# Coupled attention: queries with their turned tanh in one stack of 128 rows, and one score product per four heads

## The reference

```python
Q = split_heads(x @ Wq.T + bq)
K = split_heads(x @ Wk.T + bk)
V = split_heads(x @ Wv.T + bv)
attn_scores = jnp.einsum('bhid,bhjd->bhij', Q, K) / scale
Qn = jnp.tanh(Q)
Kn = jnp.tanh(K)
QJ = jnp.einsum('bhid,hde->bhie', Qn, J_attn)
delta = jnp.einsum('bhie,bhje->bhij', QJ, Kn)
attn_scores = attn_scores + lambda_attn * delta
attn_probs = jax.nn.softmax(attn_scores, axis=-1)
out = jnp.einsum('bhij,bhjd->bhid', attn_probs, V)
```

## Time and profile before

| | |
|---|---|
| median of 3 runs | 2906.14 us (2905.02 to 2907.65) |
| the profiled execution | 2905.46 us, of which the span is 2903.7 us |
| mean granted TensorE clock | 0.886 of full |
| TensorE busy | 2287.8 us, 79% |
| VectorE busy | 1654.6 us, 57% |
| ScalarE busy | 1354.4 us, 47% |
| GpSimd busy | 673.9 us, 23% |
| the coupled stage | about 972 to 1275 us of the span |

### The profile page before, as it was taken

How to read it: one execution, slowest core, us unless ns; L and a number is a source line. 1 busy time by engine, 2 the same in 40 slices (tenths; PEclk the granted TensorE clock), 3 DMA queues, 4 the chain that set the end, 5 groups by cost and what they waited for, 6 DMA issues and landing times. The chain is left out here.

```text
span 2903.7 us, 49967 instructions
## 1 busy us (share of the span) xinstructions
PE 2287.8 (79%) x15043; PEld 1793.6 (62%) x15043; DVE 1654.6 (57%) x4694; ACT 1354.4 (47%) x3498; POOL 673.9 (23%) x772
## 2 busy tenths in 40 slices
PE   7689999589998788869999878877777677776550
PEld 5567777479997555547777756765555555555330
DVE  2357767658885566646766767444545454533313
ACT  2166667456664455537666734433333333333210
POOL 3100000101113100010000004244444444444534
PEclk9799999899999799989999999987888878878655
DMA  3066654227662100026666431444444343433542
GB/s 98 6 154 120 123 119 106 63 88 231 206 209 77 44 1 0 0 54 134 125 123 125 96 106 49 142 135 122 132 127 138 117 130 120 120 112 115 164 150 83
DMA packets 320714, 316.71 MB, mean 109 GB/s; under 512 B 71441, under 2 KB 299746, under 8 KB 320546
## 3 DMA queue, kind: packets, MB, share of 16 engines
q1 hardware_dynamic: 296514, 261.41, 34.0%
q0 software_dynamic: 24032, 53.25, 6.3%
HBM read 209.24 MB, written 105.32 MB: 108 GB/s over the span
## 5 line engine op out<-in xcount | busy, mean ns | idle before, releaser
L793 ACT ACTIVATE cross_pr<-cross_sc,cross_mn 112x375 f32<-112x375 f32 x512 | 310.4, 606 | 233.3 <-DVE cross_mn L883 232.5
L883 DVE CUSTOM_DVE_ANT_0 cross_sc<-cross_ps,cross_masked 112x375 f32<-112x375 f32 x512 | 272.8, 543 | 179.3 <-PE cross_ps L681 158.5
L2363 POOL DMA_INDIRECT switch_slots_x<-switch_ctx,switch_slot x256 | 247.8, 968 | 492.5 <-ACT switch_ctx L2534 422.4
L2470 PE MATMUL switch_ps<-switch_ow,switch_ct 128*128 128x256 f32 x672 | 221.9, 461 | 170.4 <-ACT switch_ct L2539 89.1
L2596 DVE SCALAR_TENSOR_TENSOR switch_vt<-switch_ps,switch_chosen,switch_vt 112x128 f32<-112x128 f32 x512 | 144.2, 344 | 364.8 <-remote 162.9
L104 PE MATMUL switch_ps<-switch_vw,switchgates_xh 128*112 128x512 f32 x512 | 226.6, 442 | 103.2 <-issue 48.2
L2375 POOL DMA_INDIRECT switch_fetched<-switch_slots_y,switch_slot x256 | 240.2, 938 | 200.8 <-DVE all_x L2633 72.9
L2470 PEld LDWEIGHTS switch_ps<-switch_ow,switch_ct 128*128 128x128 f32 x672 | 143.5, 225 | 226.9 <-ACT switch_ct L2539 109.4
L689 PE MATMUL cross_ps<-all_ident,cross_pr 112*125 112x112 f32 x1536 | 256.4, 276 | 23.5 <-DVE cross_pt L890 21.9
L689 PEld LDWEIGHTS cross_ps<-all_ident,cross_pr 112*125 112x125 f32 x1536 | 234.0, 190 | 45.0 <-DVE cross_pt L890 27.7
L2544 ACT COPY switch_y_out<-switch_ps 128x512 f32<-128x512 f32 x168 | 99.9, 595 | 287.8 <-remote 179.0
(11 more groups left out here) (409 smaller groups left out, 5506.4 us busy)
## 6 DMA issues: line engine op xcount, KB each, us to landing
experts_w_raw<-in_L_ffn_w_dram SPq DMA_DIRECT2D x42, 1024.0 KB, 5.5
switch_slots_y<-switch_y_out SPq DMA_DIRECT2D x168, 256.0 KB
cross_k<-cross_k_dram SPq DMA_DIRECT2D x96, 375.0 KB, 8.1
cross_k_dram<-cross_ks SPq DMA_DIRECT2D x32, 750.0 KB, 4.5
switch_rows_in<-switch_slots_x SPq DMA_DIRECT2D x168, 128.0 KB
switch_ow<-in_L_ffn_o_w_dram SPq DMA_DIRECT2D x168, 128.0 KB
all_place<-in_ctx_dram SPq DMA_DIRECT2D x32, 375.0 KB
cross_q<-cross_q_dram SPq DMA_DIRECT2D x192, 56.0 KB, 4.4
```

What stands on the lines that cost most here:

```text
L793: nc.scalar.activation(pr[:, h % NB, :], sc[:, h % NB, :], ACT.Exp, bias=mn[parity][:, h:h + 1], scale=-1.0, accum_out=rs[parity][:, h:h + ...
L883: nc.vector.tensor_tensor_reduce(out=sc[:, h % NB, :], in0=ps[0:T, SCORES + h % 2, 0:S2], in1=mask_of[:], scale=-0.25, scalar=3e38, op0=AL ...
L2363: pool.indirect_dma_start(out=slots_x[h % 2], out_offset=at, in_=ctx[n % 2][:, j, :], in_offset=None)\
L2470: last = nc.tensor.matmul(ps[:, TILE_Y, q * D:(q + 1) * D], ct[g % 2][:, q * P:(q + 1) * P], ow[g % RING][:], start=True, stop=True)
```

## The change

The two products of a score become one. Its 128 contracted rows now hold four heads instead of eight: 64 rows with the queries of the four heads and 64 with their turned and scaled tanh; on the other side 64 rows with keys and 64 with the keys' tanh. The tile `qk` [128, 2, 2, 2, 112] holds this for queries (index 0) and keys (index 1), chunks, and halves of a chunk (i). For half 0 the plain values stand in rows 0 to 63 and the tanh in rows 64 to 127, for half 1 the other way round; `J` is put into `Jd` shifted by 64 columns, so that the turned tanh come out in the rows where they are wanted.

- VectorE adds the biases of queries and keys, in two instructions of 64 rows x 448 elements, right behind the subtraction of group 1 (line 1289 of the new file), before the sum of group 0.
- ScalarE's tanh of the queries is two instructions of 64 rows x 224 (line 1198), of the keys two more (line 1201), in group 1. The masks are four copies of 128 rows x 448 elements with the head mask as scale (line 1207), in group 2, then the turned tanh in two halves (line 1214). `o` stays behind them.
- TensorE's `scores` is one product of 448 columns (line 1098). Its other instructions are as before.
- GpSimd builds the head mask with two more small operations. SyncE's loads are the same in number.

```diff
@@ tiles @@
-        head_mask = s.sb("head_mask", [P, HP])
+        head_mask = s.sb("head_mask", [P, 2, GH])
...
-        k32 = s.sb("k32", [P, DC, T])
         qn = s.sb("qn", [P, DC, T])
-        q = [s.sb(f"q{b}", [P, DC, T]) for b in range(2)]
-        qj = [s.sb(f"qj{b}", [P, DC, T]) for b in range(2)]
-
-        km = [s.sb(f"km{b}", [P, DC, HP, T]) for b in range(2)]
-        knm = [s.sb(f"knm{b}", [P, DC, HP, T]) for b in range(2)]
+        qk = [s.sb(f"qk{b}", [P, 2, DC, 2, T]) for b in range(2)]
+        km = [s.sb(f"km{b}", [P, DC, 2, GH, T]) for b in range(2)]
@@ SyncE: where J is put @@
-                sp.dma_start(Jd[r:r + HD, h // HP, r:r + HD], J[h]).then_inc(J_loaded, 16)
+                at = (r + HALF) % P
+                sp.dma_start(Jd[r:r + HD, h // HP, at:at + HD], J[h]).then_inc(J_loaded, 16)
@@ GpSimd: head mask @@
             c.link(pool.affine_select(out=head_mask[:], in_=head_mask[:], compare_op=ALU.is_ge, fill=0.0, base=0,
-                                      pattern=[[-HD, HP]], channel_multiplier=1))
-            pool.affine_select(out=head_mask[:], in_=head_mask[:], compare_op=ALU.is_ge, fill=0.0, base=HD - 1,
-                               pattern=[[HD, HP]], channel_multiplier=-1).then_inc(const_ready, 1)
+                                      pattern=[[-HALF, 2], [-HD, GH]], channel_multiplier=1))
+            c.link(pool.affine_select(out=head_mask[:], in_=head_mask[:], compare_op=ALU.is_ge, fill=0.0, base=HD - 1,
+                                      pattern=[[HALF, 2], [HD, GH]], channel_multiplier=-1))
+            pool.tensor_tensor(head_mask[:, 0, :], head_mask[:, 0, :], head_mask[:, 1, :], ALU.add).then_inc(const_ready, 1)
@@ TensorE: scores(b, parity, g) @@
                 if g == 0:
                     pe.wait_ge(k_ready, b + 1)
-                    pe.wait_ge(tanh_ready, 2 * b + 2)
                     pe.wait_ge(qj_ready, b + 1)
                 wait(pe, shifted, b * G + g - 1)
-                c, h = g * GH // HP, g * GH % HP
-                bank = ps[0:T, SCORES + g % 2, 0:GH * T]
-                nc.tensor.matmul(bank, q[parity][:, c, :], km[parity][:, c, h:h + GH, :].rearrange("p a b -> p (a b)"),
-                                 start=True, stop=False)
-                nc.tensor.matmul(bank, qj[parity][:, c, :], knm[parity][:, c, h:h + GH, :].rearrange("p a b -> p (a b)"),
-                                 start=False, stop=True).then_inc(s_done, 1)
+                nc.tensor.matmul(ps[0:T, SCORES + g % 2, 0:GH * T], qk[parity][:, 0, g // 2, g % 2, :],
+                                 km[parity][:, g // 2, g % 2].rearrange("p a b -> p (a b)"),
+                                 start=True, stop=True).then_inc(s_done, 1)
@@ ScalarE: front(b, parity, u) @@
-                    act.wait_ge(qk_done, b + 1)
-                    wait(act, k_ready, b)
-                    wait(act, tanh_ready, 2 * b)
-                    for m in range(DC):
-                        nc.scalar.activation(q[parity][:, m, :], bank0[:, m * T:(m + 1) * T], ACT.Identity,
-                                             bias=qk_bias[:, 0, m:m + 1])
-                    for m in range(DC):
-                        last = nc.scalar.activation(k32[:, m, :], bank0[:, (DC + m) * T:(DC + m + 1) * T], ACT.Identity,
-                                                    bias=qk_bias[:, 1, m:m + 1])
-                    last.then_inc(qk_ready, 1)
                     act.wait_ge(qk_ready, b + 1)
-                    nc.scalar.activation(qn[:], q[parity][:], ACT.Tanh).then_inc(tanh_ready, 1)
-                elif u in (2, 3):
-
-                    wait(act, s_done, (b - 1) * G)
-                    for h in range((u - 2) * HP // 2, (u - 1) * HP // 2):
-                        last = nc.scalar.activation(knm[parity][:, :, h, :], k32[:], ACT.Tanh, scale=head_mask[:, h:h + 1])
-                    if u == 3:
-                        last.then_inc(tanh_ready, 1)
+                    for i in range(2):
+                        rows_of = slice(i * HALF, (i + 1) * HALF)
+                        last = nc.scalar.activation(qn[rows_of], qk[parity][rows_of, 0, :, i, :], ACT.Tanh)
+                    last.then_inc(tanh_ready, 1)
+                    for i in range(2):
+                        last = nc.scalar.activation(qk[parity][(1 - i) * HALF:(2 - i) * HALF, 1, :, i, :],
+                                                    qk[parity][i * HALF:(i + 1) * HALF, 1, :, i, :], ACT.Tanh)
+                    last.then_inc(ks_ready, 1)
+                elif u == 2:
+                    act.wait_ge(ks_ready, b + 1)
+                    for h in range(GH):
+                        last = nc.scalar.activation(km[parity][:, :, :, h, :], qk[parity][:, 1], ACT.Copy,
+                                                    scale=head_mask[:, 0, h:h + 1])
+                    last.then_inc(k_ready, 1)
                 else:
                     act.wait_ge(j_done, b + 1)
-                    nc.scalar.activation(qj[parity][:].rearrange("p a b -> p (a b)"), bank0[:, 0:DC * T], ACT.Identity,
-                                         scale=lam4[:]).then_inc(qj_ready, 1)
+                    for i in range(2):
+                        rows_of = slice((1 - i) * HALF, (2 - i) * HALF)
+                        last = nc.scalar.activation(qk[parity][rows_of, 0, :, i, :],
+                                                    bank0[rows_of, 0:DC * T].rearrange("p (a b) -> p a b", a=DC),
+                                                    ACT.Identity, scale=lam4[rows_of])
+                    last.then_inc(qj_ready, 1)
@@ ScalarE: batch @@
-                        for u in ((), (1, 2), (4, 3), ())[g]:
+                        for u in ((), (1,), (2, 3), ())[g]:
@@ VectorE: front(b, parity, u) @@
-                    dve.wait_ge(qk_ready, b + 1)
-                    for h in range(HP):
-                        last = nc.vector.tensor_scalar(km[parity][:, :, h, :], k32[:], head_mask[:, h:h + 1], None, ALU.mult)
-                    last.then_inc(k_ready, 1)
+                    dve.wait_ge(qk_done, b + 1)
+                    for i in range(2):
+                        rows_of = slice(i * HALF, (i + 1) * HALF)
+                        last = nc.vector.tensor_tensor(
+                            qk[parity][rows_of, :, :, i, :],
+                            ps[rows_of, FRONT, 0:2 * DC * T].rearrange("p (n m t) -> p n m t", n=2, m=DC),
+                            qk_bias[rows_of].unsqueeze(3).broadcast_to([HALF, 2, DC, T]), ALU.add)
+                    last.then_inc(qk_ready, 1)
@@ VectorE: batch @@
                     shift(b, g, ch)
+                    if not last and g == 1:
+                        front(b + 1, 1 - parity, 1)
                     if g >= 1:
                         total(b, parity, g - 1)
...
-                    if not last and g in (1, 2):
-                        front(b + 1, 1 - parity, g - 1)
+                    if not last and g == 1:
+                        front(b + 1, 1 - parity, 0)
```

More of the change, by code:

```diff
@@ L956, in stage_coupled_attention @@
         HP = P // HD
+        HALF = P // 2
         w = [s.sb(f"w{n}", [P, DC, D]) for n in range(4)]
@@ L993, in stage_coupled_attention @@
         xs_ready, qk_done, v_done, j_done = (s.sem(n) for n in ("xs_ready", "qk_done", "v_done", "j_done"))
-        qk_ready, tanh_ready, v_ready, qj_ready, k_ready = (s.sem(n) for n in ("qk_ready", "tanh_ready", "v_ready", "qj_ready", "k_ready"))
+        ks_ready, tanh_ready, v_ready, qj_ready, k_ready = (s.sem(n) for n in ("ks_ready", "tanh_ready", "v_ready", "qj_ready", "k_ready"))
         s_done, shifted, exped, summed, t_done, pt_ready, pv_done = (
@@ L998, in stage_coupled_attention @@
         o_ready, y_done, var_ready, rstd_ready = (s.sem(n) for n in ("o_ready", "y_done", "var_ready", "rstd_ready"))
-        xn_ready, xt_done, xt_ready, chain = (s.sem(n) for n in ("xn_ready", "xt_done", "xt_ready", "chain"))
+        xn_ready, xt_done, xt_ready, chain, qk_ready = (
+            s.sem(n) for n in ("xn_ready", "xt_done", "xt_ready", "chain", "qk_ready"))
         CHAIN = G + 5
@@ L1085, in front @@
                 else:
-                    pe.wait_ge(tanh_ready, 2 * b + 1)
+                    pe.wait_ge(tanh_ready, b + 1)
                     if isinstance(b, int) and b == 0:
@@ L1267, in batch @@
                         tail(b - 1, 1)
-            for u in (0, 1, 2, 4, 3):
+            for u in range(4):
                 front(0, 0, u)
@@ L1338, in batch @@
                         tail(b - 1, 1 - parity, 0, ch)
-                    if not last and g in (1, 2):
-                        front(b + 1, 1 - parity, g - 1)
+                    if not last and g == 1:
+                        front(b + 1, 1 - parity, 0)
                     if before and g == 3:
                         tail(b - 1, 1 - parity, 1, ch)
-            for u in range(2):
+            for u in (1, 0):
                 front(0, 0, u)
```

## The result

The changed kernel takes 2947.99 us in the median of its runs (2939.28 to 2954.82), beside 2906.89 for the kernel before on the same chips. The ratio is 1.0124, 95% interval 1.0095 to 1.0153: slower by some 36 us by the ratio; the medians lie 41 apart. The profiled execution took 2939.28 us, its span 2937.4. It is the fastest of the four, so what follows explains 33.8 us.

A forecast was written before the change was run, and what follows sets the result against it. Each batch was taken as two legs ending in waits, not bound by TensorE throughout. From 2905.5 us, +5.2 (second leg) − 3.3 (first and last batch) + 17.7 (clock) gave 2925, range 2898 to 2944.

The forecast's parts named there:

- S0's saved work: First head group's scores: one product fewer saves 0.75 us, but TensorE's wait for the normalised row grows from 0.76 to 1.51.
- first leg: Batch part from output projection to S1: a latency through VectorE and GpSimd, nothing saved, 7.52 us again.
- VectorE's adds: Two bias adds ahead of group 0's sum, 0.54 us each, eat TensorE's saved 1.5; third group's maximum 4.79 after S1.
- S1: First score product of the second head group, where the prediction cuts a batch; the four groups' scores are numbered from zero.
- ScalarE's queue: Four masked copies (2.24 us) and turned tanh (0.68) ahead of `o`: `o` at 9.91, projection 10.29 after S1, +0.37 per batch.
- The clock: TensorE's idle lump of 2.9 us before the projection brings one clock fall per batch, 1.5 us each, +17.7 us net.
- First and last batch: Ends of the stage: first batch −2.0 us from saved products, last −1.3 without adds and copies, together −3.3.
- The walk to 6.0: Last batch, without adds and copies: the projection near 6.0 us after S1 instead of 7.30, −1.3.
- second leg: Batch part from S1 to the output projection, ending in a wait for `o`: 9.92 us becomes 10.29, +5.2 over 14 batches.
- The rival of two falls per batch: The 1.5 us wait behind the first group's scores brings a second clock fall per batch: 2951 us, chance 7%.
- The clock holds: Rival: clock falls stay at about two in the stage, as before: 2907 us, no measurable difference, chance 24%.
- The rival of the shorter queue: Copies 0.48 us each, turned tanh halves 0.34 together, clock held: projection 9.63 after S1, 2898 us, chance 15%.

The follow-up runs named there:

- experiment 5: The kernel before with the second score product (the tanh part) left out, all else computed as before: 2895.8 us, ratio 0.9966 to the kernel before.
- Experiment 2: The changed kernel with unread products filling TensorE's waits, three ahead of the projection, one behind the first group's scores: 2920.9 us, ratio 1.0058 to the kernel before.
- experiment 7: The changed kernel with ScalarE's copy `o` first and two of four masked copies moved behind the second group's tanh: 2858.2 us, ratio 0.988 to the kernel before.
- experiment 3: The changed kernel with unread products ahead of the projection only, one in one kernel, three in the other: 2918.6 and 2927.4 us, stages 326.7 and 326.2.
- experiment 6: The changed kernel with the four masked key copies as VectorE multiplies instead of ScalarE copies: 2899.1 us, ratio 1.0003 to the kernel before.
- experiment 1: The changed kernel with each score product computed twice into the same bank: 2936.6 us, ratio 1.013 to the kernel before.
- 4: The changed kernel with ScalarE's copy `o` moved ahead of the masked copies and the turned tanh: 2896.8 us, ratio 0.9968 to the kernel before.
- 8: On another chip: the kernel before with `o` ahead of the tanh, 2541.7 us, ratio 0.9974; and the kernel of experiment 7 again, 2513.1 us, ratio 0.9868.

## Why the prediction came out as it did

The time, 2948 in the median and 2939.28 in the profiled execution, lies above the forecast 2925, and slower was the likeliest side. The range ended at 2944: the profiled execution is inside it, the median 4 us above. The mechanism was right; its terms were too small, and the one for the first and last batch had the wrong sign, as follows.

- *S0's saved work, first leg unchanged.* Right: 7.49 in the one first leg at full clock (forecast 7.52), and 7.52 in experiment 5.
- *VectorE's adds.* Maximum of S2 at 4.92 after S1 (1084.53), forecast 4.79, with its own queue in front of it, as said. The two adds hold VectorE 1.25, so 0.63 each, not 0.54:

```profile
L1289 DVE TENSOR_TENSOR coupled_qk<-coupled_ps,all_qk_bias 64x448 f32<-64x448 f32 x20 | 12.3, 616 | 0.1
```

  The nearer price was the upper bound, the full 0.62 of L1301.
- *ScalarE's queue.* Third exponent 6.23 (6.11), copies from 7.12 and 2.37 for four instead of 2.24, turned tanh 0.80 instead of 0.68, `o` at 10.29 (9.91), projection at 10.67 (10.29). Three steps were each low by 0.12 to 0.13 us (VectorE's adds, the four copies, the turned tanh), all in one direction, and the leg came to +0.75 instead of +0.37. Over 13 batches that is +9.8, and the forecast had +4.8. Half of 128 rows saved nothing: a tanh of 64 rows by 224 elements takes 388 ns in the mean, as its 128-row kind did (0.39 in the earlier trace rows), and the two halves of the turned tanh 442 each, as the one of 128 rows did (0.44):

```profile
L1207 ACT ACTIVATE coupled_km<-coupled_qk,coupled_head_mask 128x448 f32<-128x448 f32 x41 | 24.1, 658 | 0.0
...
L1214 ACT ACTIVATE coupled_qk<-coupled_ps,all_lam 64x224 f32<-64x224 f32 x22 | 9.7, 442 | 0.4
L1198 ACT ACTIVATE coupled_qn<-coupled_qk 64x224 f32<-64x224 f32 x20 | 7.8, 388 | 1.8 <-DVE coupled_qk L1289 1.7
```

- *The clock.* The fall once per batch came, 13 in 13 batches, with the lump of 2.89 (forecast near 3), with a mean clock of 0.81 over the 13 batches (forecast near 0.8). A warm batch would take 7.49 + 10.67 = 18.16, and 13 of them 236.1; measured are 258.95, so the falls cost 22.9, or 1.76 per batch against 1.5 forecast. Experiment 2, with one fall left, took 20.1 off the same 13 batches, without that arithmetic. Seven of the 13 falls last 10.2 us or more, through most of the first leg; the two before lasted 3.4 us, and my price came from them. Less the 3.3 of before, the term is 19.6 over 13 batches, with 16.2 forecast.
- *First and last batch.* Wrong in sign: −3.3 forecast, +1.9 measured, in two steps.
  - The first batch was to keep some 2.0 of its saved products. From first score to first projection it was 31.08 in both kernels, so it kept nothing; in experiment 5, without the longer queue, it was 28.39. And the first score itself comes 1.5 later after the stage's start. The traces show why: nothing covers the front there, and ahead of the first score the two adds, four tanh, four copies and the turned tanh stand one after another, so that it comes 10.21 us after the first projection of queries and keys where it was 8.69. GpSimd's mask is one operation more, not two, of 0.20 us, and done 9 us before the first copy reads it, so it isn't the cause.
  - The last batch's two legs took 6.40 + 7.77 where they had been 6.20 + 7.29, so +0.7 instead of −1.3. The walk to 6.0 assumed the full clock, and here a fall of 10.2 us lies over both legs. In experiment 7, where the clock was full in that batch, its second leg took 6.18.
- *Two unchanged parts* add 2.7 to the profiled difference, which nothing in the sum could hold.

By parts, forecast against profile: second leg and clock over 13 batches 21.0 against 29.3; ends −3.3 (and one batch more of both terms) against +1.9; elsewhere 0 against 2.7.

The rival of two falls per batch (2951) is near the median but isn't what happened: the trace has 13 falls with 13 lumps of 2.9, and falls on the waits behind S0 showed when that lump was filled (experiment 3). "The clock holds" would have needed 2907; with the clock held by force, experiment 2 gave 2921. The rival of the shorter queue fell with the copies at 0.59 each.

The Trainium skill (TensorE: Matmul & The Clock Gate, "Part 1: The HAM clock gate") says that the clock drops when the engine idles. The trace agrees so far as filling the waits took the falls from 13 to one in 13 batches (experiment 2). It shows no single wait above 2.9 us in these batches, and falls came with waits of at most 1.5 too (experiment 6).

What the Trainium skill (ScalarE: Activation LUTs, "Rules for kernel authors") says on multiplies, that they go to VectorE, gained 28 us of stage over the changed kernel in experiment 6 (334.2 to 305.9), but leaving them on ScalarE and changing the order gained 66.8.

Open: what decides whether the clock falls and how long it stays low. Falls in 13 batches, with the longest wait: changed kernel 13 with 2.89 us, experiment 1 nine with 2.81, 4 twelve with 2.05, the two kernels of 3 eight with 1.9 and 13 with 1.8, 6 ten with 1.5, 5 three with 1.6, 7 one with 0.94. Long waits go with falls, but the order isn't that of the lengths, nor of the sums. Open too are the few microseconds in unchanged code.

## What to carry to other kernels

Cut a loop into the legs between its handshakes and ask of each whether it is work or latency: work taken off a latency leg comes back as a wait (S0's 0.75 us here). When a change puts new instructions on an in-order queue, look at what stands behind them that someone waits for; put that first, and split the new block over the gaps that the queue already has (here +1.2% became −1.2% to −1.3%). TensorE's idle time isn't free even off the path: it cost some 20 us here through the clock. With waits of 1.8 us and more the clock fell in eight to 13 of 13 batches, but shorter pieces were no guarantee (ten falls in experiment 6, three in 5), so read the clock in a trace of each new order.

## What the hardware showed unexpectedly

Unread products made a kernel faster: filling some 3.4 us of wait per batch took the stage from 334.2 to 312.0 us. A half-height instruction of ScalarE (64 rows) takes the time of a full one: a tanh of 224 elements took 388 ns with 64 rows (L1198) and 389 with 128 (L1210 of the kernel before).

One chip ran the kernel before in 2547 us instead of 2906, and the kernel of 7 in 2513 instead of 2858. The coupled stage is equally long on both (267.6 and 267.4). The difference lies behind it, in the last stage, which took 1199 us in experiment 7 and 862 in 8. The same 100 us from the start, in 7 and then in 8:

```profile
2200.00:2300.00 100.00, 75.66 (x350) 59.42 (x348) 51.10 (x147) 37.23 (x98) 44.96 (x47) 0.87 0.46 133
```

```profile
2200.00:2300.00 100.00, 97.85 (x513) 80.12 (x512) 74.70 (x225) 52.73 (x145) 69.48 (x72) 1.00 0.63 187
```

There the DMA moved 187 GB/s instead of 133 and TensorE was busy 98% instead of 76%, at a clock of 1.00 instead of 0.87. Why that chip was faster isn't known, nor whether the transfers are the cause, so each kernel is set against the kernel before on its own chip.
